# In the odd units of the second attention, the gate projection goes ahead of the fourth scores, and the output halves go around the last values

## The reference, cut to what matters

```python
q, k, v = silu(x @ w_qkv)          # 128 columns each per head
p[s, t] = decay[s, t] * (k[s] . q[t])   # causal, 512 x 512, decay by distance
o[:, t] = sum over s of v[s] * p[s, t]
gate    = sigmoid(x @ w_gate)
out    += (gate * o) @ w_out       # summed over the 16 heads
var     = mean over all heads of o * o   # for the norm that follows
```

## Time and profile before

| | us |
|---|---|
| median of 3 runs | 1220.61 (1220.57 to 1223.69) |
| the profiled execution | 1219.5 |
| its span, first to last instruction | 1217.5 |
| TensorE matmuls busy | 1085.3 (89%) |
| VectorE busy | 918.7 (75%) |
| ScalarE busy | 730.8 (60%) |
| GpSimd busy | 393.1 (32%) |
| mean granted TensorE clock | 0.955 of full speed |

### The profile page before, as it was taken

One profiled execution on the slowest core, in us unless ns is written; L12 is line 12 of the kernel. 1 busy time (PEld: TensorE's weight loads), 2 busy tenths in 40 slices (PEclk: granted clock), 3 DMA queues, 4 the chain that ended last, 5 costly groups with the idle time before them and its releaser, 6 DMA issues. The chain is left out here.

```text
span 1217.5 us, 21634 instructions
## 1 busy us (share of the span) xinstructions
PE 1085.3 (89%) x7276; PEld 928.9 (76%) x7276; DVE 918.7 (75%) x1811; ACT 730.8 (60%) x1389; POOL 393.1 (32%) x379
## 2 busy tenths in 40 slices
PE   6779787768999999999999999999999987879995
PEld 5646555546888888888988988988988976658993
DVE  4687889847777778778778778778777786786775
ACT  5477686755666566665665656656655753535650
POOL 6365554453312112112121121121121233862440
PEclk9989798979999999999999999999999997898998
DMA  8100000119404004004004004004001001344436
GB/s 300 36 35 19 12 8 14 40 42 67 105 9 114 10 10 113 9 9 113 9 9 113 9 9 113 9 9 113 9 9 36 1 1 41 119 146 116 124 96 215
DMA packets 62325, 72.16 MB, mean 59 GB/s; under 512 B 21841, under 2 KB 49617, under 8 KB 61234
## 3 DMA queue, kind: packets, MB, share of 16 engines
q1 hardware_dynamic: 58850, 61.90, 20.8%
q0 software_dynamic: 3408, 9.39, 2.1%
HBM read 36.39 MB, written 32.78 MB: 57 GB/s over the span
## 5 line engine op out<-in xcount | busy, mean ns | idle before, releaser
L1396 PE MATMUL attn_psum<-all_h_parts,attn_wp 128*128 128x512 f32 x1152 | 300.6, 397 | 0.0
L1551 ACT CAST attn_pp<-attn_p 128x512 fp32r<-128x512 f32 (+3 forms) x256 | 117.2, 458 | 228.4 <-DVE attn_p L1645 228.3
L1396 PEld LDWEIGHTS attn_psum<-all_h_parts,attn_wp 128*128 128x128 f32 x1152 | 211.4, 189 | 40.4
L1626 DVE TENSOR_TENSOR attn_pp<-attn_p,attn_pp 128x512 fp32r<-128x512 f32 (+3 forms) x256 | 198.4, 775 | 8.1 <-ACT attn_pp L1551 8.1
L1766 POOL TENSOR_TENSOR all_gate<-all_gate,attn_sq 128x512 f32<-128x512 f32 x64 | 91.5, 1429 | 300.8 <-ACT attn_sq L1562 300.7
L1475 PE MATMUL attn_psum<-attn_qkp 128*128 128x512 f32 (+3 forms) x768 | 165.3, 325 | 4.7 <-DVE attn_qkp L1626 4.5
L1422 PE MATMUL attn_psum<-attn_pp,attn_vp 128*128 128x512 f32 (+3 forms) x768 | 163.4, 322 | 0.9 <-issue 0.5
L1422 PEld LDWEIGHTS attn_psum<-attn_pp,attn_vp 128*128 128x128 f32 x768 | 129.5, 190 | 21.1 <-issue 1.4
L1626 DVE TENSOR_TENSOR attn_yp<-attn_y,attn_yp 128x512 fp32r<-128x512 f32 x64 | 67.3, 1051 | 93.7 <-ACT attn_yp L1559 93.7
L1475 PEld LDWEIGHTS attn_psum<-attn_qkp 128*128 128x128 f32 x768 | 125.6, 191 | 13.4 <-DVE attn_qkp L1626 2.9
L1645 DVE TENSOR_TENSOR attn_p<-attn_psum,attn_mask 128x512 f32<-128x512 f32 (+3 forms) x256 | 123.8, 484 | 5.1 <-PE attn_psum L1475 3.8
(11 more groups left out here) (357 smaller groups left out, 1869.5 us busy)
## 6 DMA issues: line engine op xcount, KB each, us to landing
expert_rows<-attn_empty SPq DMA_DIRECT2D x8, 2080.0 KB, 11.4
all_wraw<-in_w1p SPq DMA_DIRECT2D x8, 1024.0 KB, 5.1
all_yacc<-expert_rows SPq DMA_DIRECT2D x39, 130.5 KB, 2.2
attn_mask<-decay_masks SPq DMA_DIRECT2D x16, 256.0 KB, 2.7
experts_wx<-expert_results SPq DMA_DIRECT2D x6, 512.0 KB, 8.4
experts_xraw<-in_wx SPq DMA_DIRECT2D x4, 608.0 KB, 4.6
all_wraw<-in_wx SPq DMA_DIRECT2D x4, 608.0 KB, 3.8
all_x<-in_x SPq DMA_DIRECT2D x4, 512.0 KB, 10.4
```

What stands on the lines that cost most here:

```text
L1396: last = nc.tensor.matmul(out, wp[:, a, k, col:col + P], hh[:, c, k, b * S:(b + 1) * S], start=(m == 0), stop=(m == 5))
L1551: nc.scalar.copy(pp[:, u % 2, 0, cols], p[:, cols]).then_inc(p_hi, 1)
L1626: nc.vector.tensor_tensor(out, whole, high.bitcast(F32), ALU.subtract).then_inc(ready, 1)
```

## The change

```diff
@@ attention1_order
     for u in range(UNITS):
-        other = "v" if u % 2 == 0 else "y"
-        order += [("s", u, 0), ("k", u), ("pv", u, 0), ("s", u, 1), ("q", u), ("pv", u, 1), ("s", u, 2), (other, u, 0),
-                  ("s", u, 3), ("pv", u, 2), (other, u, 1), ("g", u), ("pv", u, 3)]
+        order += [("s", u, 0), ("k", u), ("pv", u, 0), ("s", u, 1), ("q", u), ("pv", u, 1), ("s", u, 2)]
+        if u % 2 == 0:
+            order += [("v", u, 0), ("s", u, 3), ("pv", u, 2), ("v", u, 1), ("g", u), ("pv", u, 3)]
+        else:
+            order += [("g", u), ("s", u, 3), ("pv", u, 2), ("y", u, 0), ("pv", u, 3), ("y", u, 1)]
     return order
@@ attention1_stage, ScalarE's body
+                        if u % 2 == 1:
+                            gate_of(u, it)
                         scores_hi(u, 3, it)
                         if u % 2 == 0:
                             values_of(1, u, it)
-                        gate_of(u, it)
+                            gate_of(u, it)
```

## The result

The changed kernel takes 1237.78 us (median of 6 runs, 1236.79 to 1245.2) against 1224.99 for the kernel before in the same comparison (6 runs, 1220.57 to 1229.04). The ratio is 1.0118 with a 95% interval of 1.0083 to 1.0153, that is slower by 1.2%. The kernel before is the less steady side of the first one: three of its six runs took 1226.3 to 1229.0, and none of its 47 runs beside the experiments took more than 1223.9. The forecast was 1233, and the range of its own case 1230 to 1237; the result lies 0.8 us above that range.

A forecast was written before the change was run, and what follows sets the result against it. TensorE's matmuls, busy 1085.3 us, were taken to bound the kernel, so only its waits count. Terms 5.0 + 3.2 - 1.5 + 0.9 + 5.1 = 12.7 us on 1219.5 gave 1232.2, as median 1233; slower cases ranged 1226 to 1238.

The forecast's parts named there:

- its own case: Whole kernel: slower through waits with more half-clock stretches, 1233 us, range 1230 to 1237; chance 0.70.
- (a): Odd units: output halves move behind gate, s3 and pv2, so unit 7's 1.9 us wait for y's low part goes.
- (b): Ring order: in unit 7 s3 must wait for mask product 1; next unit 0.72 later, 5.0 us over pairs 1 to 7.
- (c): Second output half behind pv3 makes VectorE 0.45 us late; ordinary even units covered, unit 6 pays seven times: 3.2 us.
- (d): Unit 0: VectorE gets relatively earlier, which clears its wait of 0.29 us, five times: -1.5 us.
- (e): First pair: 0.6 us in unit 3 for the gate's tanh, about 0.3 in unit 5, together 0.9; last pair 0.
- a sign that it would be wrong: Ordinary even units beginning to wait before the values' matmul, L1391; at 0.2 us each it would add 5 us.
- (f): Half clock behind unit 7's waits: five of seven, three more than before, up to 1.7 us each, 5.1 us.
- The first: Unit 7: mask product 1 done about when the gate ends, both waits gone; 14 us faster, 1207; chance 0.07.
- Rival 2: Whole kernel: no measurable change, unit 6's delay caught up, half clock no more frequent, s3's wait partly given back; 1221; chance 0.05.
- Rival 3: Whole kernel: slower by the waits alone, no more half-clock stretches; 7.6 us, 1228; chance 0.18.
- The rule beside it: Unit 7: GpSimd and VectorE order untouched, so the 3.00 us stretch stays and mask 1 stays late; sum unchanged.

The follow-up runs named there:

- Experiment 1: Changed kernel, but in unit 7 VectorE makes mask product 1 before the low part of y: 1218.33 us, ratio 0.9978 to the kernel before.
- Experiment 4: Changed kernel, but in unit 7 GpSimd adds up the squares before making the low part of 1280 weight columns: 1218.59 us, ratio 0.9981.
- experiment 7: Changed kernel, but GpSimd makes the low part of only 8 of 1280 weight columns in unit 7, leaving out computation: 1208.72 us, ratio 0.9891.
- experiment 8: Changed kernel with odd tail y0 g s3 pv2 y1 pv3, the first output half ahead of the gate: 1223.46 us, ratio 1.0030.
- experiment 3: Changed kernel with odd tail g s3 pv2 y0 y1 pv3, both output halves ahead of the last values: 1231.41 us, ratio 1.0088.
- experiment 9: Changed kernel with ScalarE's order of before, the gate's tanh behind the high part of scores 3 in odd units too: 1238.19 us, ratio 1.0134.
- experiment 10: The changed kernel again, unaltered, for a second trace and more times: 1237.78 us, ratio 1.0134 to the kernel before.
- experiment 2: Kernel before, with VectorE making mask product 1 before the low part of y in unit 7: 1220.05 us, ratio 0.9987.
- experiment 5: Changed kernel with mask product 1 early in unit 7 and both output halves ahead of the last values: 1212.47 us, ratio 0.9936.
- experiment 6: Kernel before with odd tail s3 pv2 pv3 y0 y1 g, the last values ahead of both output halves: 1216.99 us, ratio 0.9971.

## Why the prediction went as it did

**The mechanism was right.** (a) The wait for the low part of y is gone. (b) Mask product 1 decides: it ended at 649.91 and s3 started 0.05 behind it. The forecast put unit 7 at 0.72 longer without half clock; pair 1 shows 13.67 against 12.87, so 0.80. Experiments 1, 4, 7 and 8 take s3's wait away in four ways, and the loss goes each time, or all but 0.3% of it. (c) Unit 6 grew by 0.48, forecast 0.45, in pairs 2 to 7; in pair 1 it grew by 0.08 only. Where it waits was only half right: the time is split between s3, which waits for its mask product there too, and the second values half. (d) Unit 0 got shorter by 0.3, as forecast. (e) Pair 1 is longer by 1.1 in unit 3 and 0.45 in unit 5 and shorter by 0.6 in unit 4, net 0.9 as forecast (0.5 and 0.45, for 0.6 and 0.3).

**The size was not, and three steps failed.** The sum gave 12.7 us on the profiled execution; it measured 17.3. Taken apart by the lengths of units:

| term | forecast | measured |
|---|---|---|
| unit 7, seven times | 5.0 | 5.7 |
| unit 6, six times 0.48 and once 0.08 | 3.2 | 3.0 |
| unit 0, pairs 2 to 7 | -1.5 | -1.5 |
| pair 1, units 3 to 5 | 0.9 | 0.9 |
| ordinary units 1 to 5, pairs 2 to 7 | 0 | 1.4 |
| half clock behind unit 7 | 5.1 | 6.4 |
| before pair 1's unit 1, pair 8 and the end | 0 | 1.4 |

The measured column is worked out: differences of start times, pair by pair; for half clock, four more stretches times 1.6, and unit 7 without them. The last row is 0.55 before unit 1 of pair 1, 0.3 in pair 8 up to its last unit, and 0.55 behind that.

1. *The cover of ordinary even units*, in (c). "0.85 of cover, enough" was read from unit 4 alone. Unit 2 has VectorE's 0.61 us for the output weights between the second addition and `gate_unit`; with them VectorE is not 0.45 late there but 0.98, which is more than the cover, and unit 2 takes 10.98 for 10.83. The prediction had named this as a sign that it would be wrong. Over six pairs it is 0.9 of the 1.4 us. The other 0.5 are hundredths in units 1, 3 and 5, in part only where modelled starts fall (last section); no run here isolates them. In experiment 3, where the second output half comes earlier, unit 2 takes no longer than unit 4, 10.86 each.
2. *Half clock*, in (f), was taken for five of seven gaps, because no wait of 2.6 us was in the trace to price it by. It came behind six, and behind seven in the traces of experiments 9 and 10. The price of one was right: 1.6 us for up to 1.7.
3. *The rest of the program* was taken at nothing, and it took 1.4 us. The start and the end of the program are not touched by the change, and no run isolates this; in pair 8, unit 2 is 0.2 us longer as in the others.

Why half clock comes so often was partly answered. Behind waits of 1.9 us it came in two pairs of seven each time (the kernel before, experiments 2 and 8), behind 2.65 us in four to seven of seven, and behind unit 7 in none where its longest wait is a few tenths (experiments 1, 4, 5 and 7) or 0.8 (experiment 6). But length alone does not decide, as experiment 3 has it behind every second of equal waits. In the changed kernel a pair with a stretch takes 92.12 us, and the next stretch falls in the same place of the next pair; in experiment 3, with other pair lengths, it alternates. That the length of the pair sets where the next one falls fits both, but it was only argued: no run changed the pair's length and kept the wait.

**Rivals.** The first, that both waits vanish, was priced at 1207. Experiment 1 made its condition true, and it gave 1218. The price was wrong by 11 us mainly because the backlog of VectorE, some 2.3 us from GpSimd's operation, does not go away when one mask product is moved: it surfaced as 0.5 in unit 7 and 0.9 in unit 0, seven times. Only taking GpSimd's operation away (experiment 7) gave 1209. Rival 2 is out, since the interval excludes no change. Rival 3, waits without more half clock, is out too: its 1228 needed as few stretches as before, and there were six.

**The rule beside it.** The Trainium skill, "GPSIMD Engine Reference", "Key points", spoke against the change: GpSimd shares its SBUF interfaces with VectorE, and VectorE operations with two SBUF inputs contend with it. Experiment 4 agrees: the stretch went from the low part of y (3.02 to 0.69) to the low part of k (0.68 to 2.96), with the mask product between them unchanged. The prediction said of the mask product that the trace agreed, but its mask product 1, at 642.14, came behind GpSimd's 2.92 us and not beside them; experiment 4 shows it. The same stretch seems to stand in the ordinary units too: the low part of scores 0, a 128x512 operation like the low part of y, takes 1.78 us beside GpSimd's 1.30 us for the squares (610.85 and 610.78 in the changed kernel). It too lies ahead of mask product 1, and no run here took it away.

## What to carry to other kernels

Where tasks share a ring of buffers, moving one changes what its neighbours wait for: look up whose buffer each task takes over in the new order, and when that reader is done in the slowest unit, not in an ordinary one. The same holds for cover: read it in each unit that has work of its own, as unit 2 has here. Where the waiting engine waits for another's backlog, a new order of the waiting one moves the wait and hardly shortens it; the gain lies in the backlogged engine's order (here one mask product in an idle gap, and the results that it waits for made earlier). When a wait becomes longer, add the half clock that may follow it to its price, by the number of places and not only by the share seen before.

## What was not expected of the hardware

Half clock can keep step with a loop. Behind equal waits of 2.66 us the changed kernel got it in pairs 2 to 7 in all three of its traces (experiment 9's with it), 92.2 us from one to the next, and experiment 3 in every second pair; each cost 1.6 us. Half clock also followed single gaps of only 1.9 us in work that was otherwise without a gap, in two places of seven.

Not everything that moves by hundredths is a cost. With the last values between the two output halves an odd unit takes 10.87 us, before it took 10.83, and with the halves side by side 10.76. But the even unit 4 behind it moves the other way: 10.79, 10.83 and 10.86. Two units together take 21.67, 21.66 and 21.62, so most of the difference lies in where the modelled start of a unit's first scores falls, and 0.05 us at most is gained by having the halves side by side.
